# Softmax sums by a matmul with ones on four column tiles, normalising and query products moved, two rounding additions moved to VectorE

## Chip, cores and metric

One core of one Trainium2 chip. The time is the device time of one execution in microseconds (us), as the median of 3 runs: 1680.28 us before the change (1679.09 to 1684.63).

## What is computed

One transformer layer in float32. Attention and feed-forward both read the same normalised input, and both are added to the residual. 16 sequences of 512 tokens, 256 features, 8 heads, latent width 64.

```
xn  = layernorm(x)
q   = xn @ Wq.T                       # 8 heads of 64
lat = xn @ Wkv_down.T                 # 64 wide
k, v = lat @ Wk_up.T, lat @ Wv_up.T   # 8 heads of 64
att = softmax(q k^T / 8) v @ Wo.T
h   = silu(fq(xn) @ fq(w_gate).T) * (fq(xn) @ fq(w_up).T)     # 704 wide
out = x + att + fq(h) @ fq(w_down).T
# fq: per 16 values, scale to max 6, round to the FP4 grid {0, .5, 1, 1.5, 2, 3, 4, 6}, scale back
```

## The kernel before, in words

The up-projections of keys and values are folded into the query and output weights once, so that all heads of a sequence share one 64-wide latent as key and value. Products that need more than one pass are built by `limbs` (line 865): each operand is split in a high and a low part, and three matmuls (hi·hi, lo·hi, hi·lo) stand for one.

**Slots.** The work is cut in 128 slots, one for each head of each sequence (8 slots in a sequence), with a lead of 14 slots, in which the weights are prepared too, and a tail of 6. Each engine has its own `slot(t)` function, and the order of the calls in it, written by hand, is the engine's order of work; semaphores join the engines. Two heads make a pair, so some steps run in even slots only (sums of softmax weights, values, layernorm statistics) and some in odd slots only (query products, normalising, down-projection, transposed input).

**TensorE, `slot` at line 1051:** query scores 0 and 1 of head t+2 (for the row maxima), gate and up products, `turn` (transposes of the quantised hidden values and of the row maxima, into bank m2), `weigh` in even slots (attention-weighted latents of a finished pair, into po), key scores 0 and 1 of head t, query products in odd slots (into m1, after a wait for VectorE's `hid`), the down-projection in odd slots (into m0), query scores 2 and 3, `weights_sum` in even slots, key scores 2 and 3, and then by slot number the latent (slot 4 of 8), its transposes (slot 6), the transposes of the next input chunk (odd slots), half of the output projection (slots 2 and 3). The query scores use two banks mx0, mx1 in turn: score qc waits until VectorE has taken the maximum of the score two before it.

**Sums.** `weights_sum` (line 1034): GpSimd has added the four key blocks of exponentials of each head of the pair into `key_sum` (128 x 2 x 512). TensorE contracts the 128 rows with a column of ones that lies beside `lat_tok`; `key_sum` is the stationary operand, 64 of its columns at a time, so 16 matmuls of one column each (2 heads x 8) write a 128 x 8 tile. VectorE takes the reciprocal (line 810) into `inv_den`, SyncE stores it to DRAM (line 419) and, after the row maxima of the slot have been placed (line 423), reads it back spread over 64 partitions for each head into `inv_b` (line 428). VectorE multiplies `po` by `inv_b` (line 787, `scaled_pair`, in the odd slot); the next pair's `weigh` waits for that.

**VectorE, `slot` at line 741:** statistics (even), maxima 0 and 1 (line 721), silu (762), hid (766), ht_lo (771), the block scales of h (693 to 698), normalising (787, odd), qp_lo (794, odd), down-projection into acc (801, odd), maxima 2 and 3, reciprocal (810, even), xn and its scales (817, even), lat, xt_lo (835, odd), output (844).

**ScalarE, `slot` at line 597:** tanh, neg_max, ht_hi, square and magic constant of h (631, 633) and of x (637, 639), on_hi, exponentials 0 and 1, qp_hi (658, odd), exponentials 2 and 3, and others.

**GpSimd, `slot` at line 518:** third addition of key_sum, on_lo, then for h of the slot before: add the magic constant (533), subtract it (535), times scale (481), and the same for x (544, 546, 481), the ratio of the next h and x (481), first two additions of key_sum (516).

**SyncE, `slot` at line 413:** all DMAs are issued on this one queue: inv_rows, neg_max, inv_b, output, high and low query parts (409, 411), residual and input loads.

Of the kernel before, what the change touches and what calls it, by code (L numbers as in the profile page):

```python
# [28 lines left out]
P = 128  # L29
# [43 lines left out]
def transformer_layer(nc, x, Wq, Wkv_down, Wk_up, Wv_up, Wo, w_gate, w_up, w_down, out):  # L73
# [6 lines left out]
    PAIRS = H // 2  # L80
    QH = 4
    CH = T // P
    KD = D // P
# [7 lines left out]
    with ExitStack() as ctx:  # L91
# [14 lines left out]
        lat1 = sb("lat1", [R + 1, 2, T], F32R)  # L106
        lat_tok = sb("lat_tok", [P, 2, CH, R + 2])
        q_hi = sb("q_hi", [P, QH, T], F32R)
# [37 lines left out]
        neg_max = sb("neg_max", [CH, 2, P], F32R)  # L146
        inv_den = sb("inv_den", [P, 2, T // R])
        stats = sb("stats", [P, 2, 6])
# [20 lines left out]

        inv_rows = nc.dram_tensor("inv_rows", (2, 2, T), F32).ap()  # L170

# [205 lines left out]
        def _(sp):  # L377
# [35 lines left out]
            def slot(t):  # L413

                m = scaled_pair(t)
                if m is not None:

                    sp.wait_ge(inv_done, m.n(1, 1))
                    sp.dma_start(inv_rows[m.c % 2].rearrange("v (p j) -> (v p) j", p=R), inv_den[:, m.c % 2, :]).then_inc(inv_stored, 16)
                u = t.plus(1)  # L420
                if u.within(SLOTS):
                    sp.wait_ge(neg_done, u.n(1, 1))
                    sp.dma_start(q_lo[R:R + 1, u.c % QH, :].bitcast(F32), neg_max[:, u.c % 2, :].bitcast(F32)).then_inc(neg_placed[u.c % 2], 16)  # L423

                if m is not None:
                    sp.wait_ge(inv_stored, m.n(16, 16))
                    for v in range(2):
                        sp.dma_start(inv_b[v * R:(v + 1) * R, :],  # L428
                                     inv_rows[m.c % 2, v:v + 1, :].broadcast_to([R, T])).then_inc(inv_spread, 16)

                m = wov_half(t.plus(-1))
                if m is not None:
                    s, j = m.over(2), m.c % 2

                    if t.i is None:
                        sp.wait_ge(out_done, m.n(1, 1))
                    sp.dma_start(out[s.value(), j * 2 * P:(j + 1) * 2 * P, :].rearrange("(c p) d -> p c d", p=P),
                                 acc[:, s.c % 2, 2 * j:2 * j + 2, :]).then_inc(out_stored[s.c % 2][j], 16)

                m = q_pair(t)  # L440
                if m is not None:
                    place_query(m, 0)

                d = t.over(2)
                if t.c % 2 == 0 and d.within(B * CH):

                    s, c = d.over(CH), d.c % CH
                    if d.c == 0:
                        sp.wait_ge(w_psum, len(JOBS))
                        sp.wait_ge(wq_done, len(WQUANT))  # L450
                    if s.c >= 2:
                        sp.wait_ge(out_stored[s.c % 2][c // 2], s.over(2).n(16))
                    sp.dma_start(acc[:, s.c % 2, c, :], x[s.value(), c * P:(c + 1) * P, :]).then_inc(res_loaded[c], 16)

                n = t.plus(19).over(2)
                if t.c % 2 and CH <= n.c < B * CH:
                    load_x(n.over(CH), n.c % CH)
                if m is not None:
                    place_query(m, 1)
# [8 lines left out]
        def _(pool):  # L468
# [49 lines left out]
            def slot(t):  # L518
# [9 lines left out]
                if w.within(SLOTS):  # L528

                    pool.wait_ge(h_magic_done, w.n(1, 1))  # L530
                    if w.any(1, -1):
                        pool.wait_ge(ht_psum, w.n(1, -1))
                    pool.tensor_tensor(h_norm[:, :], h_norm[:, :], h_magic[:, :], ALU.add).then_inc(h_round, 1)  # L533
                    pool.wait_ge(h_round, w.n(1, 1))
                    pool.tensor_tensor(h_norm[:, :], h_norm[:, :], h_magic[:, :], ALU.subtract).then_inc(h_grid, 1)  # L535
# [3 lines left out]
                if n is not None:  # L539

                    pool.wait_ge(x_magic_done, n.n(1, 1))
                    if n.any(1, -1):
                        pool.wait_ge(xt_psum, n.n(1, -1))
                    pool.tensor_tensor(x_norm[:, :], x_norm[:, :], x_magic[:, :], ALU.add).then_inc(x_round, 1)
                    pool.wait_ge(x_round, n.n(1, 1))
                    pool.tensor_tensor(x_norm[:, :], x_norm[:, :], x_magic[:, :], ALU.subtract).then_inc(x_grid, 1)
# [31 lines left out]
        def _(act):  # L578
# [18 lines left out]
            def slot(t):  # L597
# [50 lines left out]
                exp(0)  # L648
                exp(1)
                m = q_pair(t)  # L650
                if m is not None:
# [3 lines left out]
                    if m.any(1, -1):  # L655
                        for u in range(2):
                            act.wait_ge(q_hi_placed[u], m.n(2 * 16))
                    act.activation(qp_hi[:, :], m1[:, :], ACT.Copy).then_inc(q_hi_done, 1)
                exp(2)
                exp(3)  # L660
# [26 lines left out]
        def _(dve):  # L687
# [53 lines left out]
            def slot(t):  # L741
# [26 lines left out]
                if u.within(SLOTS):  # L768

                    dve.wait_ge(ht_hi_done, u.n(1, 1))  # L770
                    dve.tensor_tensor(ht_lo[:, u.c % 4, :, :], m2[:, 0:NB * P].rearrange("p (k q) -> p k q", k=NB),
                                      ht_hi[:, u.c % 4, :, :].bitcast(F32), ALU.subtract).then_inc(ht_lo_done, 1)
                if t.within(SLOTS):
                    dve.wait_ge(hid_done, t.n(1, 1))

                    if t.any(1, -1):
                        dve.wait_ge(hq_done, t.n(1, -1))
                    scales(h, h_small[:, t.c % 2, :, :], h_scales, t)
                m = scaled_pair(t)
                if m is not None:  # L780
# [6 lines left out]
                    dve.tensor_tensor(on[:, :], po[:, :], inv_b[:, :], ALU.mult).then_inc(on_done, 1)  # L787
                m = q_pair(t)
                if m is not None:
                    dve.wait_ge(q_hi_done, m.n(1, 1))  # L790
                    if m.any():
                        for u in range(2):
                            dve.wait_ge(q_lo_placed[u], m.n(16))
                    dve.tensor_tensor(qp_lo[:, :], m1[:, :], qp_hi[:, :].bitcast(F32), ALU.subtract).then_inc(q_lo_done, 1)  # L794
                d = down_chunk(t)
                if d is not None:

                    a = acc[:, d.over(CH).c % 2, d.c % CH, :]
                    dve.wait_ge(res_loaded[d.c % CH], d.over(CH).n(16, 16))
                    dve.wait_ge(down_psum, d.n(1, 1))  # L800
                    dve.tensor_tensor(a, m0[:, 0:D], a, ALU.add).then_inc(down_taken, 1)  # L801
                max_rows(t, 2)
                max_rows(t, 3)
                m = weighed_pair(t)
                if m is not None:

                    dve.wait_ge(den_psum, m.n(1, 1))
                    if m.any(1, -1):
                        dve.wait_ge(inv_stored, m.n(16, -16))
                    dve.reciprocal(inv_den[:, m.c % 2, :], m2[:, 0:T // R]).then_inc(inv_done, 1)  # L810
                if n is not None:
# [41 lines left out]
            dve.memset(hq[:, :, HALF:NB * P], 0.0).then_inc(ones_ready, 1)  # L853
            dve.memset(lat_tok[:, :, :, R:R + 2], 1.0).then_inc(ones_ready, 1)
            dve.memset(wd_hi[:, :, NB - 1, :].bitcast(F32), 0.0).then_inc(ones_ready, 1)
# [8 lines left out]
        def _(pe):  # L864
# [169 lines left out]
            def weights_sum(t):  # L1034

                m = weighed_pair(t)
                if m is not None:
                    s = m.over(PAIRS)
                    if t.plus(-2).within(SLOTS) or t.plus(1).within(SLOTS):
# [3 lines left out]
                    pe.wait_ge(sum_step, m.n(2 * (CH - 1), 2 * (CH - 1)))  # L1043
                    for j in range(T // R):
                        for v in range(2):
                            last = pe.matmul(m2[v * R:(v + 1) * R, j:j + 1],  # L1046
                                             key_sum[:, v, :].rearrange("p (q j) -> p q j", j=T // R)[:, :, j],
                                             lat_tok[:, s.c % 2, 0, R:R + 1], start=True, stop=True)
                    last.then_inc(den_psum, 1)

            def slot(t):
# [8 lines left out]
                turn(t)  # L1060
                weigh(t)
                key_scores(t, 0)
                key_scores(t, 1)
                if q_pair(t) is not None:
# [7 lines left out]
                if m is not None:  # L1072
                    b, cols = m.over(PAIRS).c % 2, slice(m.c % PAIRS * P, (m.c % PAIRS + 1) * P)
                    limbs(m1[:, :], [(wqk_hi[:, k, cols], wqk_lo[:, k, cols], xt_hi[:, b, k, :], xt_lo[:, b, k, :])
                                     for k in range(KD)]).then_inc(q_psum, 1)
                d = down_chunk(t)
                if d is not None:
# [10 lines left out]
                query_scores(t, 3)  # L1088
                weights_sum(t)
                key_scores(t, 2)  # L1090
# [86 lines left out]
```

## Time and profile before

| | before |
|---|---|
| median of 3 runs | 1680.28 us (1679.09 to 1684.63) |
| the profiled execution: its time | 1681.53 us |
| its span, first to last instruction | 1679.7 us |
| mean granted TensorE clock | 0.935 of full speed |
| busy in the span: TensorE, VectorE, ScalarE, GpSimd | 93%, 63%, 43%, 72% |

The profile shows one execution. PE is TensorE's matmuls, PEld its weight loads (they overlap PE), DVE is VectorE, ACT ScalarE, POOL GpSimd, SPq SyncE's DMA queue. L1046 is line 1046 of the kernel before. Idle time is put down to what ended it. The ends of matmuls are modelled, so a busy share of PE near 100% does not say that it ran at full rate; the granted clock (PEclk, 1.0 is 2.4 GHz, 0.5 is 1.2 GHz) must be read beside it. A float32 matmul stands as two instructions in these rows.

### The profile page before, as it was taken

How to read it: one execution, taken by the hardware profiler on the slowest of the kernel's cores; microseconds unless marked ns; L12 is line 12 of the kernel's file. 1: busy time of each engine (PE TensorE's matmuls, PEld its weight loads, DVE VectorE, ACT ScalarE, POOL GpSimd, SP SyncE). 2: the span in 40 equal slices, each digit the busy share in tenths (PEclk: the TensorE clock that was granted, in tenths of full speed). 3: DMA queues.
4: the chain of work that ended last, by engine and by line, in shares of the span. 5: the costliest groups of instructions: out<-in, count | busy, mean ns of one | idle time of the engine just before them, and what ended most of it. 6: DMA issues, size and time to landing. Idle time of an engine off the chain costs nothing.

```text
span 1679.7 us, 28564 instructions
## 1 busy us (share of the span) xinstructions
PE 1557.5 (93%) x9446; PEld 1214.1 (72%) x9446; DVE 1052.3 (63%) x2472; ACT 716.5 (43%) x1574; POOL 1214.2 (72%) x1336
## 2 busy tenths in 40 slices
PE   1489999999999999999999999999999999999997
PEld 1366787777778777777877777777777777787676
DVE  7677666666666666666566656756666675655452
ACT  3444444344444444444444443434444443444332
POOL 7568867777787777778687776868777776765664
PEclk9789999989999899999999998999999999998998
DMA  3022222221222122122122212212222221221210
GB/s 111 22 54 62 64 60 52 73 56 49 69 64 62 47 76 61 41 71 64 52 58 76 59 50 65 61 48 64 67 54 52 77 63 46 58 61 42 55 51 26
DMA packets 82273, 98.27 MB, mean 59 GB/s; under 512 B 21712, under 2 KB 48848, under 8 KB 82128
## 3 DMA queue, kind: packets, MB, share of 16 engines
q1 hardware_dynamic: 82128, 96.45, 22.2%
q8 instruction: 77, 1.26, 0.3%
q14 instruction: 68, 0.56, 0.1%
HBM read 37.16 MB, written 8.65 MB: 27 GB/s over the span
## 4 chain that ended last, share of the span: by engine, by line
PE 71%; DMA 9%; DVE 7%; ACT 4%; issue 3%; SPq 3%; POOL 2%; POOLq 0%; DVEq 0%; ACTq 0%
PE m L869 28%; PE po L1030 13%; PE m L1046 8%; PE mx L969 7%; DMA inv_b<-inv_rows 7%; PE st L997 6%; PE st L998 4%; PE m L981 2%; DMA q_hi<-qp_hi 2%; DVE qp_lo L794 1%; DVE row_max L721 1%; SPq L423 1%; SPq L428 1%; ACT neg_max L622 1%; PE m L985 1%
## 5 line engine op out<-in xcount | busy, mean ns | idle before, releaser
L606 ACT ACTIVATE probs<-st 128x512 f32<-128x512 f32 x512 | 279.7, 593 | 425.6 <-PE st L998 425.4
L721 DVE TENSOR_REDUCE row_max<-mx 128x1 f32<-128x512 f32 x512 | 328.2, 682 | 136.7 <-PE mx L969 135.8
L516 POOL TENSOR_TENSOR key_sum<-key_sum,probs 128x512 f32<-128x512 f32 x256 | 328.7, 1284 | 37.8 <-ACT probs L606 1.8
L1030 PE MATMUL po<-probs,lat_tok 128*64 128x512 f32 x1024 | 233.8, 598 | 0.0
L969 PE MATMUL mx<-lat,q_hi 128*128 128x512 f32 x512 | 188.6, 437 | 46.9 <-DVE row_max L721 32.0
L997 PE MATMUL st<-q_hi,lat 128*128 128x512 f32 x512 | 232.0, 453 | 0.1
L998 PE MATMUL st<-q_lo,lat 65*128 65x512 f32 x512 | 213.5, 417 | 0.0
L614 ACT ACTIVATE hid<-m 128x352 f32<-128x352 f32 x128 | 59.4, 464 | 319.8 <-PE m L869 319.8
L533 POOL TENSOR_TENSOR h_norm<-h_norm,h_magic 128x352 f32<-128x352 f32 x128 | 110.0, 859 | 115.3 <-ACT h_magic L633 115.3
L869 PE MATMUL m<-wgu_hi,xt_hi 128*128 128x352 f32 x512 | 180.4, 352 | 1.9 <-DVE acc L801 1.0
L526 POOL TENSOR_TENSOR on_lo<-on,on_hi 128x512 fp32r<-128x512 f32 x64 | 81.7, 1277 | 137.6 <-ACT on_hi L647 137.6
L869 PE MATMUL m<-wgu_lo,xt_hi 128*128 128x352 f32 x512 | 177.9, 348 | 0.0
L869 PE MATMUL m<-wgu_hi,xt_lo 128*128 128x352 f32 x512 | 176.7, 345 | 0.0
L516 POOL TENSOR_TENSOR key_sum<-probs 128x512 f32<-128x512 f32 x128 | 164.2, 1282 | 2.5 <-PE m L1046 2.5
L1030 PEld LDWEIGHTS po<-probs,lat_tok 128*64 128x64 f32 x1024 | 67.8, 136 | 123.9 <-issue 123.9
L969 PEld LDWEIGHTS mx<-lat,q_hi 128*128 128x128 f32 x512 | 94.4, 200 | 83.1 <-DMA q_hi<-qp_hi 41.4
L997 PEld LDWEIGHTS st<-q_hi,lat 128*128 128x128 f32 x512 | 101.4, 198 | 69.5 <-issue 51.3
L1046 PEld LDWEIGHTS m<-lat_tok,key_sum 128*64 128x64 f32 x2048 | 128.2, 216 | 24.5 <-issue 24.5
L1046 PE MATMUL m<-lat_tok,key_sum 128*64 128x1 f32 x2048 | 133.6, 259 | 0.8 <-POOL key_sum L516 0.8
L787 DVE TENSOR_TENSOR on<-po,inv_b 128x512 f32<-128x512 f32 x64 | 44.2, 691 | 121.0 <-DMA inv_b<-inv_rows 121.0
L535 POOL TENSOR_TENSOR h_norm<-h_norm,h_magic 128x352 f32<-128x352 f32 x128 | 110.0, 859 | 10.0
L869 PEld LDWEIGHTS m<-wgu_hi,xt_hi 128*128 128x128 f32 x512 | 108.6, 212 | 9.9 <-ACT lat L665 3.8
(179 smaller groups left out, 3511.4 us busy)
## 6 DMA issues: line engine op xcount, KB each, us to landing
q_hi<-qp_hi SPq DMA_DIRECT2D x256, 128.0 KB, 2.3
q_lo<-qp_lo SPq DMA_DIRECT2D x128, 128.0 KB, 2.3
inv_b<-inv_rows SPq DMA_DIRECT2D x128, 128.0 KB, 2.9
x_in<-in_L_attn_x_dram SPq DMA_DIRECT2D x64, 128.0 KB, 2.3
acc<-in_L_attn_x_dram SPq DMA_DIRECT2D x64, 128.0 KB, 2.1
out_dram<-acc SPq DMA_DIRECT2D x32, 256.0 KB, 2.9
q_lo<-neg_max SPq DMA_DIRECT2D x128, 2.0 KB
inv_rows<-inv_den SPq DMA_DIRECT2D x64, 4.0 KB, 1.4
```

The costliest lines, as they stand in the source:

```text
L516: pool.tensor_tensor(total, first, last, ALU.add).then_inc(sum_step, 1)
L526: pool.tensor_tensor(on_lo[:, m.c % PAIRS, :], on[:, :], on_hi[:, m.c % PAIRS, :].bitcast(F32), ALU.subtract).then_inc(on_lo_done, 1)
L533: pool.tensor_tensor(h_norm[:, :], h_norm[:, :], h_magic[:, :], ALU.add).then_inc(h_round, 1)
L535: pool.tensor_tensor(h_norm[:, :], h_norm[:, :], h_magic[:, :], ALU.subtract).then_inc(h_grid, 1)
L606: act.activation(probs[:, t.c % 2, kc, :], st[kc % 2][:, :], ACT.Exp).then_inc(exp_done, 1)
L721: dve.tensor_reduce(row_max[:, u.c % 2, qc:qc + 1], mx[qc % 2][:, :], AX.X, ALU.max).then_inc(mx_taken, 1)
L869: last = pe.matmul(dst, a, b, start=(n == 0), stop=(n == len(ms) - 1))
L969: pe.matmul(mx[qc % 2][:, :], q_hi[:, u.c % QH, qc * P:(qc + 1) * P], lat[:, s.c % 2, :], start=True, stop=True).then_inc(mx_psum, 1)
L997: pe.matmul(st[kc % 2][:, :], lat[:, s.c % 2, keys], q_hi[:, h, :], start=True, stop=False)
L998: pe.matmul(st[kc % 2][:, :], lat1[:, s.c % 2, keys], q_lo[:, h, :], start=False, stop=True).then_inc(st_psum, 1)
L1030: last = pe.matmul(po[v * R:(v + 1) * R, :], lat_tok[:, s.c % 2, kc, 0:R], probs[:, v, kc, :], start=(kc == 0), stop=(kc == CH - 1))
L1046: last = pe.matmul(m2[v * R:(v + 1) * R, j:j + 1], key_sum[:, v, :].rearrange("p (q j) -> p q j", j=T // R)[:, :, j], lat_tok[:, s.c % 2, ...
```

## The change

Four edits:

- `weights_sum` uses a tile of ones (128 x 32) as the stationary operand and `key_sum` as the moving one, 256 columns at a time: 4 float32 matmuls, each on 32 columns of the array, so 32 partitions of m2 and 256 columns for each half head. The reciprocal is then over 128 x 256, and 4 of its rows, 32 partitions apart, are stored (4 rows of 1 KB). On TensorE the sums stand right behind `weigh`, before key scores 0.
- Query products on TensorE stand before key scores 1, and qp_hi on ScalarE before exponential 1.
- On VectorE, normalising moves from before qp_lo to behind maxima 2 and 3 (odd slots), and the reciprocal from behind them to before them (even slots).
- The additions of the magic constants of h (every slot) and x (odd slots) go from GpSimd to VectorE, ahead of the block scales of h. GpSimd waits for their results.

```
 # VectorE slot, new order
+                w = t.plus(-1)
+                r = norm_chunk(w)
+                if w.within(SLOTS):
+                    dve.wait_ge(h_norm_done, w.n(1, 1))
+                    dve.wait_ge(h_magic_done, w.n(1, 1))
+                    dve.tensor_tensor(h_norm[:, :], h_norm[:, :], h_magic[:, :], ALU.add).then_inc(h_round, 1)
+                if r is not None:
+                    dve.wait_ge(x_norm_done, r.n(1, 1))
+                    dve.wait_ge(x_magic_done, r.n(1, 1))
+                    dve.tensor_tensor(x_norm[:, :], x_norm[:, :], x_magic[:, :], ALU.add).then_inc(x_round, 1)
...
                     scales(h, h_small[:, t.c % 2, :, :], h_scales, t)
...
+                    dve.reciprocal(inv_den[:, m.c % 2, :], m2[:, 0:T // 2]).then_inc(inv_done, 1)
...
+                max_rows(t, 2)
+                max_rows(t, 3)
                 m = scaled_pair(t)
...
 # GpSimd slot
-                    pool.wait_ge(h_magic_done, w.n(1, 1))
+                    pool.wait_ge(h_round, w.n(1, 1))
...
-                    pool.tensor_tensor(h_norm[:, :], h_norm[:, :], h_magic[:, :], ALU.add).then_inc(h_round, 1)
-                    pool.wait_ge(h_round, w.n(1, 1))
...
 # TensorE, weights_sum
-                    for j in range(T // R):
-                        for v in range(2):
-                            last = pe.matmul(m2[v * R:(v + 1) * R, j:j + 1],
-                                             key_sum[:, v, :].rearrange("p (q j) -> p q j", j=T // R)[:, :, j],
-                                             lat_tok[:, s.c % 2, 0, R:R + 1], start=True, stop=True)
+                    for k in range(4):
+                        last = pe.matmul(m2[k * QR:(k + 1) * QR, 0:T // 2], ones[:, :],
+                                         key_sum[:, k // 2, k % 2 * T // 2:(k % 2 + 1) * T // 2], start=True, stop=True)
...
 # TensorE slot
                 weigh(t)
+                weights_sum(t)
                 key_scores(t, 0)
-                key_scores(t, 1)
...
                     limbs(m1[:, :], [(wqk_hi[:, k, cols], wqk_lo[:, k, cols], xt_hi[:, b, k, :], xt_lo[:, b, k, :])
                                      for k in range(KD)]).then_inc(q_psum, 1)
+                key_scores(t, 1)
...
                 query_scores(t, 3)
-                weights_sum(t)
...
 # SyncE
-                    sp.dma_start(inv_rows[m.c % 2].rearrange("v (p j) -> (v p) j", p=R), inv_den[:, m.c % 2, :]).then_inc(inv_stored, 16)
+                    sp.dma_start(inv_rows[m.c % 2], inv_den[0:P:QR, m.c % 2, :]).then_inc(inv_stored, 16)
```

## Rows read from the trace of the kernel before

**Rows 1.** The page: busy time, granted clock in 40 slices

```profile
PE 1557.5 (93%) x9446; PEld 1214.1 (72%) x9446; DVE 1052.3 (63%) x2472; ACT 716.5 (43%) x1574; POOL 1214.2 (72%) x1336
...
PEclk9789999989999899999999998999999999998998
```

**Rows 2.** Windows: length, busy PE PEld DVE ACT POOL, granted clock, DMA share, GB/s

```profile
0.00:108.00 108.00, 45.80 (x185) 34.77 (x185) 73.62 (x216) 43.45 (x98) 64.15 (x100) 0.84 0.23 64
183.70:185.80 2.10, 2.10 (x34) 2.04 (x33) 1.21 (x2) 0.31 (x1) 2.02 (x4) 1.00 0.00 0
186.60:190.00 3.40, 3.40 (x12) 3.12 (x11) 1.98 (x6) 1.30 (x3) 2.39 (x3) 0.50 0.02 1
207.30:1592.00 1384.70, 1341.54 (x8195) 1047.96 (x8194) 875.99 (x2030) 600.85 (x1320) 1019.44 (x1101) 0.94 0.23 59
1657.80:1668.00 10.20, 7.65 (x35) 7.41 (x36) 1.67 (x3) 1.12 (x2) 1.97 (x2) 0.50 0.10 28
```

**Rows 3.** Chain of waits around one pair: start, length, what

```profile
788.25 0.61 DVE row_max L721
...
792.35 3.58 PE po L1030 x16
...
797.53 2.02 PE m L1046 x32
```

**Rows 4.** Groups by line and shape: busy us, mean ns, idle before

```profile
L810 DVE RECIPROCAL inv_den<-m 128x8 f32<-128x8 f32 x64 | 13.2, 207 | 70.1 <-PE m L1046 70.1
L698 DVE RECIPROCAL x_small<-x_small 128x16 f32<-128x16 f32 x64 | 16.2, 253 | 0.0
L698 DVE RECIPROCAL h_small<-h_small 128x22 f32<-128x22 f32 x130 | 37.5, 289 | 0.0
L533 POOL TENSOR_TENSOR h_norm<-h_norm,h_magic 128x352 f32<-128x352 f32 x128 | 110.0, 859 | 115.3 <-ACT h_magic L633 115.3
L516 POOL TENSOR_TENSOR key_sum<-key_sum,probs 128x512 f32<-128x512 f32 x256 | 328.7, 1284 | 37.8 <-ACT probs L606 1.8
```

**Rows 5.** Single lines: count, duration ns min/median/max

```profile
L739 DVE TENSOR_TENSOR h_norm<-h_norm,w_magic x8: 361/611/1378, 13.5 to 61.7; 128x256 f32<-128x256 f32 x6, 128x352 f32<-128x352 f32 x2
L695 DVE TENSOR_SCALAR h_small<-h_small x136: 174/390/1218, 11.1 to 1647.1; 128x22 f32<-128x22 f32 x130, 128x16 f32<-128x16 f32 x5, 64x16 f32<-64x16 f32 x1
```

**Rows 6.** Waits: who waited for whom, us in total, times, longest

```profile
DVE on L787 <- DMA inv_b<-inv_rows: 121.0, 63, 3.4
PE mx L969 <- DVE row_max L721: 32.0, 33, 1.8
PE mx L969 <- DMA q_hi<-qp_hi: 11.4, 16, 2.2
...
PEld mx L969 <- DMA q_hi<-qp_hi: 41.4, 43, 2.4
PEld mx L969 <- DVE row_max L721: 17.4, 47, 1.6
PEld m L869 <- DVE hid L766: 15.6, 28, 0.8
```

**Rows 7.** Timeline of an odd slot and the even one behind it: start, length, instruction

```profile
783.73 0.86 POOL L533 TENSOR_TENSOR h_norm<-h_norm,h_magic 128x352 f32<-128x352 f32 x1 [0.83 <-ACT h_magic L633]
783.79 0.84 DVE L695 TENSOR_SCALAR h_small<-h_small 128x22 f32<-128x22 f32 x1
...
788.00 0.38 PE L1125 MATMUL m<-ident,xq 128*128 128x128 f32 x2
...
788.99 1.00 PE L969 MATMUL mx<-lat,q_hi 128*128 128x512 f32 x2 [0.60 <-DVE row_max L721]
...
789.83 0.32 PE L869 MATMUL m<-wgu_hi,xt_hi 128*128 128x352 f32 x1
...
790.62 2.75 POOL L516 TENSOR_TENSOR key_sum<-key_sum,probs 128x512 f32<-128x512 f32 x2
...
793.05 0.56 DVE L771 TENSOR_TENSOR ht_lo<-m,ht_hi 128x384 fp32r<-128x384 f32 x1
```

More of the change, by code:

```diff
@@ L81, in transformer_layer @@
     QH = 4
+    QR = P // 4
     CH = T // P
@@ L106, in transformer_layer @@
         lat1 = sb("lat1", [R + 1, 2, T], F32R)
-        lat_tok = sb("lat_tok", [P, 2, CH, R + 2])
+        lat_tok = sb("lat_tok", [P, 2, CH, R])
         q_hi = sb("q_hi", [P, QH, T], F32R)
@@ L146, in transformer_layer @@
         neg_max = sb("neg_max", [CH, 2, P], F32R)
-        inv_den = sb("inv_den", [P, 2, T // R])
+        inv_den = sb("inv_den", [P, 2, T // 2])
+        ones = sb("ones", [P, QR])
         stats = sb("stats", [P, 2, 6])
@@ L168, in transformer_layer @@
         wo_t = pflat[:, o1:o1 + PAIRS * D].rearrange("p (n d) -> p n d", d=D)
-        inv_rows = nc.dram_tensor("inv_rows", (2, 2, T), F32).ap()
+        inv_rows = nc.dram_tensor("inv_rows", (2, 4, T // 2), F32).ap()
         def psum(name):
@@ L428, in slot @@
                         sp.dma_start(inv_b[v * R:(v + 1) * R, :],
-                                     inv_rows[m.c % 2, v:v + 1, :].broadcast_to([R, T])).then_inc(inv_spread, 16)
+                                     inv_rows[m.c % 2, 2 * v:2 * v + 2, :].rearrange("k q -> (k q)").unsqueeze(0).broadcast_to([R, T])).then_inc(inv_spread, 16)
                 m = wov_half(t.plus(-1))
@@ L539, in slot @@
                 if n is not None:
-                    pool.wait_ge(x_magic_done, n.n(1, 1))
+                    pool.wait_ge(x_round, n.n(1, 1))
                     if n.any(1, -1):
                         pool.wait_ge(xt_psum, n.n(1, -1))
-                    pool.tensor_tensor(x_norm[:, :], x_norm[:, :], x_magic[:, :], ALU.add).then_inc(x_round, 1)
-                    pool.wait_ge(x_round, n.n(1, 1))
                     pool.tensor_tensor(x_norm[:, :], x_norm[:, :], x_magic[:, :], ALU.subtract).then_inc(x_grid, 1)
@@ L648, in slot @@
                 exp(0)
-                exp(1)
                 m = q_pair(t)
@@ L658, in slot @@
                     act.activation(qp_hi[:, :], m1[:, :], ACT.Copy).then_inc(q_hi_done, 1)
+                exp(1)
                 exp(2)
@@ L778, in slot @@
                     scales(h, h_small[:, t.c % 2, :, :], h_scales, t)
+                m = q_pair(t)
+                if m is not None:
+                    dve.wait_ge(q_hi_done, m.n(1, 1))
+                    if m.any():
+                        for u in range(2):
+                            dve.wait_ge(q_lo_placed[u], m.n(16))
+                    dve.tensor_tensor(qp_lo[:, :], m1[:, :], qp_hi[:, :].bitcast(F32), ALU.subtract).then_inc(q_lo_done, 1)
+                m = weighed_pair(t)
+                if m is not None:
+                    dve.wait_ge(den_psum, m.n(1, 1))
+                    if m.any(1, -1):
+                        dve.wait_ge(inv_stored, m.n(16, -16))
+                    dve.reciprocal(inv_den[:, m.c % 2, :], m2[:, 0:T // 2]).then_inc(inv_done, 1)
+                d = down_chunk(t)
+                if d is not None:
+                    a = acc[:, d.over(CH).c % 2, d.c % CH, :]
+                    dve.wait_ge(res_loaded[d.c % CH], d.over(CH).n(16, 16))
+                    dve.wait_ge(down_psum, d.n(1, 1))
+                    dve.tensor_tensor(a, m0[:, 0:D], a, ALU.add).then_inc(down_taken, 1)
+                max_rows(t, 2)
+                max_rows(t, 3)
                 m = scaled_pair(t)
@@ L787, in slot @@
                     dve.tensor_tensor(on[:, :], po[:, :], inv_b[:, :], ALU.mult).then_inc(on_done, 1)
[L788 to L810, printed above, removed]
                 if n is not None:
@@ L853, in _ @@
             dve.memset(hq[:, :, HALF:NB * P], 0.0).then_inc(ones_ready, 1)
-            dve.memset(lat_tok[:, :, :, R:R + 2], 1.0).then_inc(ones_ready, 1)
+            dve.memset(ones[:, :], 1.0).then_inc(ones_ready, 1)
             dve.memset(wd_hi[:, :, NB - 1, :].bitcast(F32), 0.0).then_inc(ones_ready, 1)
@@ L1037, in weights_sum @@
                 if m is not None:
-                    s = m.over(PAIRS)
                     if t.plus(-2).within(SLOTS) or t.plus(1).within(SLOTS):
```

## The prediction

> **What bounds the kernel now.** I began with the page's busy shares and its row of granted clock [rows 1]. TensorE is busy for 93% of the span; no other engine is above 72%. But the clock row hardly ever shows full speed, and the mean granted clock is 0.935. So two things are to be priced: work on TensorE, and the speed at which it runs. The windows [rows 2] give the second. From 207.3 to 1592.0 us, 56 pairs of heads in 1384.7 us (24.7 us a pair), the clock averages 0.94. Half clock loses half of a stretch's work, so the whole execution loses 0.065 x 1679.7 = 109 us, 0.16 x 108 = 17 us of it in the lead: 92 us are lost in the pairs, 1.4 us each. What stands before the falls is the same thing nearly each time: the sum step, then half clock. The second and third row of that group are the first case, the last row is the last (10.2 us at 0.50 in the tail); I count 45 such stretches after the lead, 40 of them behind a sum step. In the chain of waits the sum step is 2.02 us of 32 instructions on one-column operands [rows 3], while the values step before it (512 columns, 3.58 us) leaves the clock alone. The sum step thus costs 2.02 us for itself and about 1.25 us in what follows.
>
> Then TensorE's own waits [rows 6]. Three matter: VectorE's row maxima, the query DMA and `hid`. Counting only idle matmuls they are 32.0 + 11.4 = 43 us, counting idle weight loads (41.4 + 17.4 + 15.6) too 118 us. In the timeline the last transposes start at 788.00 and the next slot's gate at 789.83 [rows 7]; transposes and two scores need 0.2 + 0.47 us of that, so some 1.2 us are lost where the rows mark 0.60 as idle. I take about twice the idle, 90 us over 64 pairs (1.4 each). Its cause is visible there: VectorE stood 1.9 us for `inv_b` in the mean, 121.0 us in all [rows 6], and the maxima were queued behind it.
>
> **Part 1, the sum step.** 4 float32 matmuls are 8 instructions of 256 columns. The nearest row is the values step: 16 instructions of 512 columns on two column tiles in 3.58 us [rows 3], so 0.45 us for two instructions side by side, 0.224 us for a pair of 256 columns. Low bound: all four tiles side by side, 2 x 0.224 = 0.45 us. High bound: nothing overlaps, 8 x 0.21 = 1.7 us. I take two at a time, as that row shows, with some 0.1 us to drain: 1.0 us. Saved 1.02 x 64 = **65 us** (20 to 100). For this case of tiles of 32 columns the Trainium skill, TensorEngine Tiling (Array Packing), Theoretical Speedup, allows up to 4x; by it the step would be the low bound, and 35 us more would be saved. The step's place right behind the values adds no wait: key_sum's last addition ended at 793.4 us and ht_lo, the last reader of m2, at 793.6 [rows 7], 2.3 us before the values step did [rows 3].
>
> **Part 2, the clock.** One-column instructions go; in their place stand 256-column ones like the ones around them. Low bound of the gain: nothing (some fall comes from waits, which remain). High: 92 us. Five falls of 45 had no sum step ahead, and new waits may add some, so I take **80 us**.
>
> **Part 3, VectorE's additions.** Reciprocal: 207 ns for 8 elements, 253 for 16, 289 for 22 [rows 4], 5.9 ns an element. For 256 that is 0.25 + 240 x 0.0059 = 1.7 us; bounds 0.45 us (one element per cycle, as the 512-column maxima in 0.61 us go [rows 3]) and 2.0. Added 1.5 us a pair. Magic additions: no such row in the slots, but the weights' addition is the same operation [rows 5]: 361 ns at least for 256 elements, so 0.46 for 352; 1378 at most. Uncontended that is 0.46 + 0.46 + 0.36 = 1.28 us a pair. VectorE has 876.0 / 56 = 15.6 us a pair now [rows 2]; with 2.8 more it is 18.4, below the 22.4 us that I forecast. GpSimd loses 0.86 + 0.86 + 0.68 us a pair and has slack: priced at nothing.
>
> What the additions wait for is dearer. A 22-element tensor_scalar takes 174 ns, but 1218 at most and 390 in the median [rows 5]; one of 0.84 us ends just as GpSimd's 0.86 us addition ends [rows 7]. The Trainium skill, SBUF — State Buffer, Who interferes with whom, speaks against this edit: an instruction with two SBUF inputs, as these additions are, waits out a whole GpSimd instruction, for the port pair is locked. By it each addition could cost up to 1.3 us more. I take 0.5 us a slot, so that VectorE needs some 19.4 us a pair.
>
> **Part 4, where VectorE now holds TensorE.** (Lengths of stretches are added up from single instructions of the timeline, like those of rows 3, 4 and 7.) *After the even slot's sum.* Sum end to last maximum: 0.15 + 1.7 + 1.25 = 3.1 us. TensorE has key scores 0 to 3 and query scores 2, 3 and 0, 2.57 us, before it needs that bank: 0.55 us lost, in the plain quarter of the pairs, less with transposes, none where the output projection or the latent follows: 13 us. *At the query products.* After that last maximum VectorE does xn and its scales (1.3), maxima 0, 1 (1.28), silu and hid (2 x 0.53), 3.65 us; TensorE has 3.1 us up to the moved products (key scores 1 no longer cover the wait): 0.6 us in half of the pairs, 19 us. *At the end of the odd slot.* From hid to the last maximum VectorE has ht_lo, two additions with their waits, scales, qp_lo, acc, maxima: 6.3 to 6.8 us; TensorE 5.9: 0.9 us in three quarters, 43 us. *Query DMA:* products come 0.47 us and qp_hi another 0.54 us earlier on ScalarE, so the 53 us [rows 6] fall to 10. Sum 85 us, against 90 today: **no change**, between 45 us less (VectorE fast, no port waits) and 65 us more (1 us more a pair). The 121 us wait for inv_b goes: inv_b lands, by SyncE's order, before maxima 2 and 3 are through. Late next is not that DMA but VectorE's own queue. Nothing waits early for the normalised pair: the next values step comes a half slot later. SyncE issues as many DMAs as before in the same order; the store has 4 rows instead of 128, which sits beside other work: nothing, either way.
>
> **Sum.** 1681.5 (this execution; 1679.7 in its span) - 65 - 80 - 0 = 1536.5; the median of the runs lies 1.3 us lower, so **1535 us**, 22.4 us a pair. By the page's fourfold packing it would be 1500.
>
> **Rivals.**
> - *Full packing, VectorE hides.* The four tiles run together, all of the clock returns, waits fall by 45 us: 1681.5 - 100 - 92 - 45 = 1445. For it: the values step's two tiles do overlap. Against: 2.8 us more for VectorE. Chance 0.14.
> - *The tiles don't do what they say:* one after another, 1.7 us. Then 20 + 80 saved: 1580. No row has 32-column tiles. Chance 0.12.
> - *The clock does not return.* The falls are merely moved to the new waits behind reciprocal and hid: 65 + 15: 1600. Five falls without a sum speak for it, 40 with one against. Chance 0.12.
> - *VectorE becomes the bound* by port waits of about 1 us at each addition: 23.7 us a pair, 1 us x 64 less gain plus: 1615. Chance 0.10.
> - *Slower.* The place is VectorE's two additions and the tensor_scalars behind them: if each addition waits out a 1.28 us GpSimd addition [rows 4] and the tensor_scalars go from 0.39 to 1.2 us, a pair takes 15.6 + 1.5 + 1.28 + 3 x 1.28 + 2 x 0.8 = 23.8 us, with 1.4 us of waits that VectorE can't avoid (for the sum, for the constants) 25.2, that is 32 us more than today: 1713. It decides from 24.7 us a pair on. GpSimd stood idle 115.3 us before just these additions [rows 4], so it is mostly not in the port then. Chance 0.06.
>
> **How the numbers follow.** The forecast has 0.46 with its own range of 1500 to 1570. From 1470 to 1615 the range leaves out most of full packing, half of VectorE's bound and the slower case, and takes in the bounds of the sum step (-35, +45) with part of those of the clock. Faster, slower and same are told apart at 0.3%, 5 us, about what a measurement can tell here. Only the slower case and strips of two others end above: faster 0.92, same 0.02, slower 0.06.
>
> **What would show it.** Right: the sum step near 1.0 us on 8 instructions a pair; granted clock at 0.98 or more after the lead; the reciprocal at 1.7 us; DVE busy near 1240 us, POOL near 1060; the wait for inv_b all but gone; waits of TensorE for row_max or hid still 40 to 90 us. Wrong: half-clock stretches as many as before (part 2), magic additions over 1 us in the mean (part 3), or a pair above 23.5 us with TensorE waiting for maxima.

## The result, and the profile after

Median 1501.65 us (1498.06 to 1504.18, 4 runs) against 1679.68 us (1666.06 to 1684.63, 4 runs): a ratio of 0.895, 95% interval 0.8895 to 0.9006. The forecast was 1535 us in 1470 to 1615.

| | before | after |
|---|---|---|
| the profiled execution: its time, its span | 1681.53, 1679.7 us | 1504.18, 1502.4 us |
| mean granted TensorE clock | 0.935 | 0.979 |
| busy: PE, DVE, POOL | 1557.5, 1052.3, 1214.2 us | 1391.0, 1262.6, 1074.5 us |

The chain of waits of the kernel before, by engine (shares of the span):

```profile
PE 71%; DMA 9%; DVE 7%; ACT 4%; issue 3%; SPq 3%; POOL 2%; POOLq 0%; DVEq 0%; ACTq 0%
```

The page after, its row of the granted clock (to be held against [rows 1]) and its chain:

```profile
PEclk9679999999999999999999999999999999999998
...
PE 65%; DVE 24%; issue 4%; ACT 3%; POOL 2%; DMA 1%; SPq 1%; DVEq 0%; POOLq 0%; ACTq 0%
```

The clock row shows no dent left between lead and tail. In the clock record of the trace, half-clock time between 108 us and the last 60 us is 3.4 us after and 167 us before (41 stretches). And VectorE, 7% of the chain before, holds 24% of it now. The groups (busy us, mean ns, idle before):

```profile
L1052 PE MATMUL m<-key_sum,ones 128*32 128x256 f32 x512 | 40.9, 391 | 1.2 <-POOL key_sum L518 1.2
L800 DVE RECIPROCAL inv_den<-m 128x256 f32<-128x256 f32 x64 | 111.4, 1740 | 19.2 <-PE m L1052 19.2
L776 DVE TENSOR_TENSOR h_norm<-h_norm,h_magic 128x352 f32<-128x352 f32 x128 | 92.3, 721 | 24.5 <-ACT h_magic L631 24.5
L780 DVE TENSOR_TENSOR x_norm<-x_norm,x_magic 128x256 f32<-128x256 f32 x64 | 54.3, 849 | 11.4 <-ACT x_magic L637 9.9
```

The sum step is 8 instructions, and in the chain of waits it is short; the key scores behind it follow at once:

```profile
718.87 3.58 PE po L1038 x16
722.45 0.57 PE m L1052 x8
723.02 0.43 PE st L1005
```

0.57 us, where it was 2.02 [rows 3]. The waits of TensorE after, against [rows 6]:

```profile
PEld m L877 <- DVE hid L764: 47.6, 62, 1.3
...
PE m L877 <- DVE hid L764: 17.4, 31, 0.8
...
PEld mx L977 <- DVE row_max L719: 15.3, 49, 1.8
...
PE mx L977 <- DVE row_max L719: 12.3, 16, 1.4
...
PEld mx L977 <- DMA q_hi<-qp_hi: 7.6, 7, 1.6
...
PE mx L977 <- DMA q_hi<-qp_hi: 4.3, 5, 1.2
```

The wait for hid has grown from 15.6 us of idle weight loads to 47.6, those for the maxima and the query DMA have fallen, and the 121 us that VectorE stood for inv_b do not appear any more. Where one figure is given for a wait of TensorE below (65 us for hid, 28 for the maxima, 12 for the query DMA here), idle matmuls (PE) and idle weight loads (PEld) are added; a moment in which both are idle then counts twice, so such figures are for comparing kernels and are not a price.

### The profile page after: what moved, and what is told of

Read it like the earlier page. It is cut to its first block, busy times and chain, and to the rows that moved or that the text cites. A ratio compares the mean times of both kernels' runs of the same rounds, so it can differ in the third digit from the quotient of the medians.

```text
span 1502.4 us, 25684 instructions
## 1 busy us (share of the span) xinstructions
PE 1391.0 (93%) x7910; PEld 1022.6 (68%) x7910; DVE 1262.6 (84%) x2664; ACT 715.3 (48%) x1574; POOL 1074.5 (72%) x1144
## 4 chain that ended last, share of the span: by engine, by line
PE 65%; DVE 24%; issue 4%; ACT 3%; POOL 2%; DMA 1%; SPq 1%; DVEq 0%; POOLq 0%; ACTq 0%
PE m L877 32%; PE po L1038 12%; DVE row_max L719 6%; PE mx L977 6%; PE st L1005 5%; PE st L1006 5%; DVE inv_den L800 2%; DVE hid L760 2%; DVE hid L764 2%; PE m L1052 2%; PE m L989 1%; PE m L1130 1%; DVE rstd L751 1%; DMA q_hi<-qp_hi 1%; DVE x_small L691 1%
## 5 line engine op out<-in xcount | busy, mean ns | idle before, releaser
L1005 PE MATMUL st<-q_hi,lat 128*128 128x512 f32 x512 | 217.2, 424 | 0.4 <-ACT probs L604 0.4
L1006 PE MATMUL st<-q_lo,lat 65*128 65x512 f32 x512 | 203.0, 397 | 0.0
L877 PE MATMUL m<-wgu_hi,xt_hi 128*128 128x352 f32 x512 | 169.0, 330 | 2.6
L877 PE MATMUL m<-wgu_lo,xt_hi 128*128 128x352 f32 x512 | 166.4, 325 | 0.0
L535 POOL TENSOR_TENSOR h_norm<-h_norm,h_magic 128x352 f32<-128x352 f32 x128 | 115.6, 903 | 57.3 <-DVE h_norm L776 57.3
L483 POOL TENSOR_TENSOR x_norm<-xn,x_small 128x256 f32<-128x256 f32 x64 | 39.8, 622 | 131.6 <-DVE x_small L696 131.3
L800 DVE RECIPROCAL inv_den<-m 128x256 f32<-128x256 f32 x64 | 111.4, 1740 | 19.2 <-PE m L1052 19.2
L776 DVE TENSOR_TENSOR h_norm<-h_norm,h_magic 128x352 f32<-128x352 f32 x128 | 92.3, 721 | 24.5 <-ACT h_magic L631 24.5
L877 PE MATMUL m<-wd_hi,ht_hi 128*128 128x256 f32 x384 | 108.9, 284 | 0.8 <-DVE acc L852 0.8
L483 POOL TENSOR_TENSOR hq<-h_norm,h_small 128x352 f32<-128x352 f32 x128 | 102.3, 799 | 10.0
```

The source lines that it names most:

```text
L483: return pool.tensor_tensor(blocks(dst), blocks(src), per_block.unsqueeze(2).broadcast_to([rows, cols // BLOCK, BLOCK]), ALU.mult)
L776: dve.tensor_tensor(h_norm[:, :], h_norm[:, :], h_magic[:, :], ALU.add).then_inc(h_round, 1)
L800: dve.reciprocal(inv_den[:, m.c % 2, :], m2[:, 0:T // 2]).then_inc(inv_done, 1)
L877: last = pe.matmul(dst, a, b, start=(n == 0), stop=(n == len(ms) - 1))
L1005: pe.matmul(st[kc % 2][:, :], lat[:, s.c % 2, keys], q_hi[:, h, :], start=True, stop=False)
L1006: pe.matmul(st[kc % 2][:, :], lat1[:, s.c % 2, keys], q_lo[:, h, :], start=False, stop=True).then_inc(st_psum, 1)
```

## The experiments

My theory: the sum step and the half clock behind it carry the gain, the rest is worth little. The rival: the moves carry a good part. The first two runs put the step and the rest apart. The kernel before was run again with every group of experiments, with medians from 1675 to 1680 us, so a difference of about 5 us between runs of different groups says little.

**The new sum step alone**, in the kernel before, at its old places:

```
-                    for j in range(T // R):
-                        for v in range(2):
...
+                    for k in range(4):
+                        last = pe.matmul(m2[k * QR:(k + 1) * QR, 0:T // 2], ones[:, :],
+                                         key_sum[:, k // 2, k % 2 * T // 2:(k % 2 + 1) * T // 2], start=True, stop=True)
```

> The kernel before with the new sum step alone (ones on four column tiles, reciprocal over 256 columns, 4-row store), at its old places in the slot. Theory A (the sum step and the clock it cost carry the gain; the moves and the additions are worth little): the step falls from 2.02 to about 0.57 us, 64 x 1.45 = 93 us, the half-clock stretches behind it go, 75 to 90 us, and the longer reciprocal sits behind the last maxima where nobody waits: 1500 to 1530 us, granted clock 0.97 or more. Theory B (the moves carry a good part: TensorE becomes faster than the chain over inv_b, on which VectorE still waits ahead of its maxima): inv_b is waited for longer than before (over 121 us, the reciprocal being 1.5 us longer) and the time stays above 1560 us.

Measured: 1531.31 us, ratio 0.9137 (0.9099 to 0.9176), clock 0.981. That is 1 us above theory A's range, with 6.8 us of half clock between lead and tail; but theory B's mechanism is in it as well, VectorE still stands for inv_b:

```profile
DVE on L789 <- DMA inv_b<-inv_rows: 100.6, 64, 3.2
```

**The old sum step in the changed kernel**, at the new place:

```
-                    for k in range(4):
...
+                    for j in range(T // R):
+                        for v in range(2):
+                            last = pe.matmul(m2[v * R:(v + 1) * R, j:j + 1],
```

> The changed kernel with the one-column sum step of the kernel before (2 us, reciprocal over 8 columns, 128-row store) at the new place behind the values step; all moves and the additions on VectorE stay. Theory A: the step costs 1.45 us more and brings its half-clock stretches back, while the short reciprocal gives VectorE 1.5 us a pair: 1502 + 93 + 75 - 15 = about 1650 us, granted clock 0.93 to 0.95. Theory B: moves and additions carry a good part, so this stays below 1610 us.

Measured: 1579.62 us, ratio 0.9427 (0.9377 to 0.9478), clock 0.965. Theory A fails here by 70 us. With one-column sums the rest of the change is worth 1679.7 - 1579.6 = 100 us, with the new ones 1531.3 - 1501.7 = 30 us. So the parts do not add: step 148 us alone, rest 100 us alone, both 178 us, 70 us less than the sum. Most of what they share is the clock: half-clock time between lead and tail is 58 us in this run, against 167 before, although the one-column instructions are all there; that is (167 - 58) / 2 = 54 us of TensorE's work that either part gives back, but only once. The old step is also shorter here, 1.80 us for 2.02 in the chain of waits, which makes another 14 us.

**Only the old step's place changed**, in the kernel before:

```
                 weigh(t)
+                weights_sum(t)
                 key_scores(t, 0)
...
                 query_scores(t, 3)
-                weights_sum(t)
```

> The kernel before with its one-column sum step only moved on TensorE, right behind the values step; nothing else is changed. Theory A (where the step stands decides how often the clock falls: with it here, the changed kernel with one-column sums had 17 half-clock stretches between lead and tail against 41): half-clock time falls from 167 to 50 to 90 us and the time by 25 to 50 us, to 1630 to 1655. Theory B (the fewer falls there came from the other edits): 150 us or more of half clock, time within 10 us of 1680.

Measured: 1627.88 us, ratio 0.9668 (0.962 to 0.9717), half-clock time 92 us in 27 stretches. Theory A holds. The windows of a like stretch (length, busy PE PEld DVE ACT POOL, granted clock, DMA share, GB/s), first the kernel before, then this one:

```profile
200.00:1440.00 1240.00, 1204.46 (x7385) 939.36 (x7384) 796.88 (x1864) 543.11 (x1194) 925.16 (x1004) 0.94 0.23 60
```

```profile
200.00:1440.00 1240.00, 1202.91 (x7665) 944.82 (x7665) 830.55 (x1934) 565.45 (x1244) 964.58 (x1050) 0.97 0.24 63
```

and the step in its chain of waits:

```profile
705.41 3.58 PE po L1030 x16
708.99 1.81 PE m L1046 x31
710.80 0.43 PE st L997
```

0.97 for 0.94, and the step itself 1.81 instead of 2.02 us. (167 - 92) / 2 = 37 us of clock and 64 x 0.21 = 13 us of the step make 50 of the 52 us, if each us of TensorE's time counts in full. One line of TensorE's order is worth 3%.

**The step made long, with the clock kept.** Four times the same 4 matmuls:

```
-                    for k in range(4):
+                    for k in [k for _ in range(4) for k in range(4)]:
```

> The changed kernel with the 4 matmuls of the sum step done 4 times over (same result). The step grows from 0.57 us to some 2.0 us, as long as the one-column step, but on 256-column operands. Theory A: the clock stays at 0.97 or more, TensorE is the bound and each us counts: 1502 + 64 x 1.45 = 1595 us, less 10 to 20 where TensorE would have waited anyway. Theory B (VectorE is the bound): under 40 us slower. Against the one-column step at the same place, the difference between the two is the price of the clock: 60 to 90 us.

Measured: 1569.78 us, ratio 0.9369 (0.9331 to 0.9407), no half clock between lead and tail. In its chain of waits:

```profile
749.33 1.86 PE m L1052 x32
```

The step takes 1.86 to 1.91 us in the chain, some 1.3 us more, 83 us in all; the time rose by 68: so each us of the step counts 0.8 us. That is less than theory A's 1575 to 1585, and well over theory B's 1542: TensorE is the bound, with some slack. The 60 to 90 us that I expected against the one-column step of equal length are only 10. The comparison was not a clean one: that run had 58 us of half clock (29 us lost, not 75), and its reciprocal was 1.5 us a pair shorter, which the run with a short reciprocal below puts at 22 us. 29 - 22 = 7 us is near to the 10 measured.

**All on one column tile** (`inv_den` is filled with ones once, at the start, so that the rows that are left out have a value):

```
-                        last = pe.matmul(m2[k * QR:(k + 1) * QR, 0:T // 2], ones[:, :],
+                        last = pe.matmul(m2[0:QR, 0:T // 2], ones[:, :],
...
-                    dve.reciprocal(inv_den[:, m.c % 2, :], m2[:, 0:T // 2]).then_inc(inv_done, 1)
+                    dve.reciprocal(inv_den[0:QR, m.c % 2, :], m2[0:QR, 0:T // 2]).then_inc(inv_done, 1)
```

> The changed kernel with all 4 matmuls of the sum step on the same column tile and the same 32 rows of m2; three of the four quarters of the sums are left out, the reciprocal runs over 32 rows, 256 columns. Theory A (the step is 0.57 us because the four tiles run side by side): 8 instructions in a row, 8 x 0.21 = 1.7 us, and the time rises by 0.82 us per us of the step, as the fourfold step did: 1502 + 64 x 1.13 x 0.82 = 1561. Theory B (256-column float32 instructions of 32 columns are short in themselves): under 0.8 us.

Measured: 1569.04 us, ratio 0.934 (0.929 to 0.9391). The same 8 instructions, in its chain of waits:

```profile
725.92 1.86 PE m L1053 x8
```

1.86 us on one tile, 0.57 on four: 3.3 times. Theory A. The fourfold step above says it more sharply: 32 such instructions on four tiles took 1.86 us, as long as 8 on one tile, so four tiles do four times the work in the same time, and the 3.3 has a fixed part of some 0.1 us in it. The Trainium skill, TensorEngine Tiling (Array Packing), Theoretical Speedup, allows up to 4x for a dimension of at most 32; the traces agree, with 3.3 for the step as it is and 4.0 for the fourfold one. The price that I took, two tiles at a time, came from a row of 64-column tiles and was the wrong one to go by.

Next, the rest of the change, edit by edit, each undone in the changed kernel.

**Normalising back ahead of qp_lo:**

```
+                m = scaled_pair(t)
...
                 m = q_pair(t)
...
                 max_rows(t, 2)
                 max_rows(t, 3)
-                m = scaled_pair(t)
```

> The changed kernel with normalising back ahead of qp_lo. Theory A (this move carries most of the 30 us by which the rest of the change beats the new sum step alone): VectorE waits for inv_b again, 60 us or more in all, the maxima come late, and the time rises by 15 to 35 us, 1517 to 1537. Theory B (inv_b lands early enough since the sums come earlier in the slot): within 6 us of 1502.

Measured: 1533.02 us, ratio 0.9119 (0.9058 to 0.9181): 31 us slower. The time is theory A's; the mechanism only in part, since VectorE waits 22 us for inv_b, not 60:

```profile
PE mx L977 <- DVE row_max L719: 26.4, 47, 1.7
PEld mx L977 <- DVE row_max L719: 24.2, 66, 1.6
DVE inv_den L809 <- PE m L1052: 22.5, 48, 3.4
DVE on L795 <- DMA inv_b<-inv_rows: 22.0, 21, 2.9
```

TensorE's waits for maxima go from 28 to 51 us; its idle matmuls alone, which can't count twice, show 14 of the 31 us. My reading is that even with inv_b there, the 0.68 us product stands ahead of the maxima that TensorE needs, while nobody needs the product soon; where the rest of the 31 us went the rows don't say.

**Reciprocal back behind the maxima:**

```
-                    dve.reciprocal(inv_den[:, m.c % 2, :], m2[:, 0:T // 2]).then_inc(inv_done, 1)
...
                 max_rows(t, 2)
                 max_rows(t, 3)
+                    dve.reciprocal(inv_den[:, m.c % 2, :], m2[:, 0:T // 2]).then_inc(inv_done, 1)
```

> The changed kernel with the reciprocal back behind maxima 2 and 3; all else stays. Theory A (the 1.74 us reciprocal ahead of the maxima holds up the query scores of the next slot): TensorE's waits for row_max shrink from 28 us to under 10 and the time falls by 8 to 20 us, 1482 to 1494. Theory B (the order is indifferent, since VectorE's total is what counts): within 4 us of 1502.

Measured: 1548.51 us, ratio 0.921 (0.9136 to 0.9284): 47 us slower. Both theories fall. The waits show why:

```profile
PEld m L877 <- DVE hid L764: 72.1, 62, 2.1
...
DVE row_max L719 <- PE mx L977: 55.1, 64, 1.9
...
PE m L877 <- DVE hid L764: 43.5, 47, 1.7
```

and VectorE's timeline (start, length):

```profile
726.77 0.29 DVE L696 RECIPROCAL h_small<-h_small 128x22 f32<-128x22 f32 x1
727.50 1.29 DVE L719 TENSOR_REDUCE row_max<-mx 128x1 f32<-128x512 f32 x2 [0.43 <-PE mx L977]
728.71 1.75 DVE L809 RECIPROCAL inv_den<-m 128x256 f32<-128x256 f32 x1
```

Right behind the sum TensorE has key scores to do, and until it has done them VectorE has no query scores to reduce: now it stands idle there, once in each pair, 55 us in all. In the changed kernel the reciprocal fills just that gap, and the maxima wait 1.5 us in the whole run:

```profile
L719 DVE TENSOR_REDUCE row_max<-mx 128x1 f32<-128x512 f32 x512 | 322.9, 672 | 2.1 <-PE mx L977 1.5
```

Moved behind, it comes before the next slot's maxima 0 and 1 and hid, and the query products wait for hid 50 us more (26 of them idle matmuls). I had counted the reciprocal as what stood ahead of the maxima, and not asked what VectorE would do without it there.

A part of the 47 us is the clock again. Between lead and tail this run has 30.7 us at half clock in 9 stretches, where the changed kernel has 3.4: 14 us lost. All 9 stand right behind a wait of TensorE for hid of 1.7 us; one of them (the matmul behind the wait, then the windows of the wait, of the 1 us behind it and of the fall: length, busy PE PEld DVE ACT POOL, granted clock, DMA share, GB/s):

```profile
461.81 0.50 PE L877 MATMUL m<-xt_hi,wqk_hi 128*128 128x512 f32 x1 [1.69 <-DVE hid L764]
```

```profile
460.00:461.80 1.80, 0.12 (x1) 0.00 (x0) 1.70 (x5) 1.74 (x5) 1.66 (x3) 1.00 0.03 6
461.80:462.80 1.00, 0.99 (x4) 0.86 (x5) 1.00 (x2) 0.68 (x2) 1.00 (x1) 1.00 0.43 80
462.90:466.10 3.20, 3.20 (x13) 2.81 (x12) 3.17 (x7) 1.19 (x2) 2.98 (x4) 0.50 0.26 80
```

So a wait can cost more than its own length. Six further waits of 1.7 us in this run had no fall behind them.

**A short reciprocal** (`inv_den` filled with ones once, at the start):

```
-                    dve.reciprocal(inv_den[:, m.c % 2, :], m2[:, 0:T // 2]).then_inc(inv_done, 1)
+                    dve.reciprocal(inv_den[:, m.c % 2, 0:8], m2[:, 0:8]).then_inc(inv_done, 1)
```

> The changed kernel with a reciprocal over 8 of the 256 columns (the other weights' sums are not inverted: the normalising factors are left out for them). VectorE loses 64 x 1.53 = 98 us of busy time. Theory A (VectorE is a second bound beside TensorE): 20 to 45 us faster, 1457 to 1482, with TensorE's waits for row_max and hid under half. Theory B (TensorE is the bound, VectorE's load is hidden): under 10 us.

Measured: 1479.86 us, ratio 0.8806 (0.8747 to 0.8866): 22 us less, for 94 us less VectorE work. Inside theory A's range at its edge, but the waits for hid stayed (47.9 and 17.9 us) and those for the maxima fell only from 28 to 17, so its account of them is wrong. VectorE's work counts about 0.23 us per us there.

**The additions back on GpSimd:**

> The changed kernel with the additions of the magic constants back on GpSimd. VectorE loses 92 + 54 us of busy time. Theory A (VectorE, at 84% busy, is what TensorE now waits for; GpSimd has slack): faster by 10 to 30 us, 1472 to 1492. Theory B (the additions were moved because GpSimd's chain to hq and key_sum is near the path): slower by 10 to 30 us, 1512 to 1532.

The edit is the reverse of the diff's first two parts. Measured: 1496.26 us (1495.77 to 1497.9), ratio 0.8933 (0.8897 to 0.8969). Neither: some 5 us faster, as much as groups of runs differ by, and the intervals of the ratios overlap, so I take it as no change. 74 us less work for VectorE and 138 us more for GpSimd cancel nearly: TensorE's waits for the maxima fall from 28 to 13 us, and those for hid rise from 65 to 80.

**Query products and qp_hi back at their places:**

```
                 key_scores(t, 0)
+                key_scores(t, 1)
...
-                key_scores(t, 1)
                 d = down_chunk(t)
...
                 exp(0)
+                exp(1)
```

> The changed kernel with key scores 1 back ahead of the query products and exponential 1 ahead of qp_hi. Theory A (the move shortens the way from the products to the query DMA that the next slot's scores wait for): the wait for that DMA rises from 12 us to 40 or more, the wait for hid falls from 65 us to 20, net 5 to 20 us slower. Theory B (the wait for hid, which key scores 1 covered, weighs more): 5 to 15 us faster.

Measured: 1489.45 us (1488.43 to 1491.27), ratio 0.8864 (0.8805 to 0.8924): 12 us faster. (The interval of the ratio overlaps a little with that of the changed kernel, 0.8895 to 0.9006; both hold the spread of the kernel before. The runs themselves are 7 us apart at the nearest.) The time is theory B's, and both mechanisms are there:

```profile
PEld mx L977 <- DMA q_hi<-qp_hi: 35.4, 49, 2.4
...
PE mx L977 <- DMA q_hi<-qp_hi: 21.3, 43, 2.2
PEld m L877 <- DVE hid L764: 16.4, 31, 0.8
...
PEld mx L977 <- DVE row_max L719: 8.6, 22, 1.6
...
PE m L877 <- DVE hid L764: 5.5, 15, 0.4
...
PE mx L977 <- DVE row_max L719: 2.9, 5, 1.1
```

The DMA wait rose from 12 to 57 us and the wait for hid fell from 65 to 22, so these two cancel, and by the rows B's does not weigh more. What is left is a wait that neither theory named: the one for the maxima fell from 28 to 12 us. Why it did was not tested.

**Both undone**, additions and query edit:

> The changed kernel with two of its edits undone together: magic additions back on GpSimd, key scores 1 and exponential 1 back at their old places. What stays is the new sum step and its place, and normalising behind the maxima. Theory A (the two edits each cost something by VectorE's queue ahead of hid and independently): the gains of the two single runs add, 5 + 12 us: 1483 to 1487. Theory B (they relieve the same wait, for hid): no better than the query edit undone alone, 1489 us.

Measured: 1492.34 us (1489.83 to 1494.79), ratio 0.8883 (0.8856 to 0.891): theory B by its time, the single gains don't add. TensorE waits 28 us for hid and 50 for the query DMA.

**The same, with exponential 1 left behind qp_hi**, so that of the query edit only TensorE's half is undone:

> As the run with additions and key scores 1 back, but exponential 1 stays behind qp_hi on ScalarE, as in the changed kernel. Theory A (undoing both halves of the query edit made TensorE wait 57 us for the query DMA; ScalarE's half alone brings qp_hi 0.5 us earlier): that wait falls under 40 us and the time is 3 to 10 us below the run with both halves undone. Theory B (exponential 1 held back stalls key scores 3 as much): within 3 us.

Measured: 1482.6 us (1480.02 to 1483.99), ratio 0.8825 (0.8798 to 0.8852). Theory A: 10 us less than with both halves undone, and the wait for the query DMA falls from 50 to 13 us. Its waits:

```profile
PEld m L871 <- DVE hid L768: 27.0, 45, 1.1
...
PEld mx L971 <- DMA q_hi<-qp_hi: 8.5, 18, 1.5
PE mx L971 <- DMA q_hi<-qp_hi: 4.2, 8, 1.2
```

The wait for hid, 37 us, is between the two extremes of 65 and 22, and the one for the DMA is as short as in the changed kernel. The same half with the additions left on VectorE was not run. This kernel computes the same and is faster than both kernels of the study, by 1.3% against the changed one.

## Why the prediction was right, point by point

- **Part 1, the sum step: right kind, wrong size.** I took 1.0 us, between 0.45 and 1.7; it is 0.57, near the low bound. Taken full, that is 93 us instead of 65. The one-tile run shows both the high bound (1.86) and that the tiles run side by side. By the two lengthened steps a us of it is worth 0.8 us, so 75 us are nearer to what it gave. The price was mis-sized because it took two tiles side by side where four ran.
- **Part 2, the clock: 80 us predicted.** The mean clock over the span gives 0.065 x 1679.7 = 109 us lost before and 0.021 x 1502.4 = 32 us after: 77 us back. (My 92 us for the pairs had 8 us of the tail in it: by the clock record 167 / 2 = 84 were lost between lead and tail, of which 82 came back, and the lead lost 5 more.) The reason that I gave, the one-column instructions, was enough: with the new operands at the old place half-clock time was 6.8 us. Of the 41 falls between lead and tail, 36 had no idle time of TensorE just ahead of them and 5 stood behind a wait of 1.6 to 1.8 us for the maxima; the rival by which waits keep the clock down had a true mechanism, as the 9 falls of the run with the reciprocal moved back show, but the changed kernel has one wait of TensorE of 1.4 us there and none longer. What I did not see is that the place counts too: the old instructions at the new place lose 37 us less, and with the other edits 54 us less ((167 - 58) / 2).
- **Part 3, VectorE.** Reciprocal 1.74 us for 1.7 forecast: the line through 8, 16 and 22 elements [rows 4] held to 256. Busy time 1262.6 us for 1240, GpSimd's 1074.5 for 1060. The additions took 0.72 and 0.85 us, with 0.515 and 0.410 at least:

```profile
L776 DVE TENSOR_TENSOR h_norm<-h_norm,h_magic x128: 515/526/1622, 104.7 to 1472.8; 128x352 f32<-128x352 f32 x128
...
L780 DVE TENSOR_TENSOR x_norm<-x_norm,x_magic x64: 410/991/1515, 7.7 to 1323.0; 128x256 f32<-128x256 f32 x64
```

  146.6 - 128 x 0.515 - 64 x 0.41 = 54 us of waiting, 0.42 us a slot for the 0.5 that I took. The maximum, 1.62 us, is the minimum and 1.1 us more, less than one key_sum addition of 1.29. The Trainium skill, SBUF — State Buffer, Who interferes with whom, says that an instruction with two SBUF inputs contends with a GpSimd instruction that reads SBUF, and that the shared ports are an exclusive lock. The trace agrees: 48 of the 128 h additions and 40 of the 64 x additions were over 0.06 us longer than the shortest, a GpSimd instruction ran at the start of each of them, and they ended 0.38 us (h) and 0.28 us (x) after it did, within 0.01 us each time. So GpSimd was mostly out of the way for the h addition (median 0.526 us) and mostly in the way for the x addition (median 0.991), which my reading of its idle time had not told apart.
- **Part 4, the waits.** Their sum was forecast as unchanged, and that came out near by luck: two errors of opposite sign met in it. Idle matmuls for maxima, hid and query DMA were 49 us and are 34; with idle weight loads 123 and 104. What I had wrong is their make-up: hid has 65 us of it (19 forecast), the maxima 28 (56 forecast), the query DMA 12 (10 forecast). (My 90 us for today were idle matmuls taken twice and my 85 were added up from stretches, so neither is the same measure as these rows.) I had hid waited for in half of the pairs; there are 62 such waits in 64 pairs. That moving the query products would cost is what this term should have said: undone, they give 12 us back.
- **The sum.** With the measured terms, 1681.5 - 93 - 77 = 1511.5 us against 1504.2 of the profiled execution: 7 us are left for the waits. The forecast was 32 us above that execution, 28 of them from the size of part 1. The case "full packing" had that right, but it gave the waits 45 us.
- **Not in the forecast at all:** that normalising ahead of the maxima would cost 31 us in this kernel. I had its wait for inv_b gone and nobody waiting early for its result, but put no gain beside it, since it was set off against the new load. Nor that the reciprocal's new place is worth 47 us, 14 of them by the clock.

## What to carry to other kernels

Look at the granted clock beside busy shares: a busy engine may have run at half speed because of a 2 us step in front of it, and that step may be cured by its shape or by its place; a wait of TensorE of 1.7 us can have the same thing behind it, so moving an instruction on another engine can cost clock as well. Before moving an instruction out of the way of something urgent, find what its engine would do in that time; a long one belongs where the engine has nothing to do. Undo the edits of a change that is a success one at a time, because one of the four here cost 12 us and another gave nothing that could be told from noise, and then by halves: of the edit that cost time, ScalarE's half was worth 10 us where TensorE's half was undone.

## What the runs showed of the hardware that I had not expected

- How often the clock fell hung on what stood around the one-column step: 167 us at half clock with query scores ahead of it and key scores behind, 92 with the values step ahead, 58 with the other edits too. In all three TensorE had no idle time just ahead of most falls; 5 of 41, 4 of 27 and 1 of 17 stood behind a wait of 1.4 us or more. Why the neighbours matter was not settled.
- The one-column step itself was shorter behind the values step, 1.81 against 2.02 us. This is open too.
- The first key score behind the values or the sum step takes 0.43 us in the chain, the next ones 0.23 to 0.24, at full clock, and a first key score behind a query score or the gate products also takes 0.23: 0.2 us more where TensorE comes from tiles of 32 or 64 columns to 128. That the tiles are the cause was not tested.
